# Two diagonals for the slots' maxima, POOL started by VectorE's first tile, and token maxima broadcast through DRAM in a soft-MoE dispatch

## What is computed

```
xn = rmsnorm(x, norm_gamma);  sn = rmsnorm(slot_embeds, slot_norm_gamma)
logits = einsum('bnd,esd->bnes', xn, sn)              # 2048 tokens x (8 experts x 128 slots)
dispatch = softmax(logits, axis=1)                    # over the tokens, one sum for each slot
combine = softmax(logits.reshape(b, n, e * s), -1)    # over the slots, one sum for each token
slots = einsum('bnd,bnes->besd', xn, dispatch)
h = gelu(einsum('besd,edh->besh', slots, w1) + b1)
eo = einsum('besh,ehd->besd', h, w2) + b2
out = einsum('bmd,bnm->bnd', eo, combine)
```

## Time and profile before

| what | value |
|---|---|
| time, median of 3 runs | 3299.77 us (3297.85 to 3300.67) |
| profiled execution | 3297.0 us |
| its span in the trace | 3295.2 us |
| mean granted clock of PE | 0.981 |
| busy: PE, PEld, DVE, ACT, POOL | 93%, 47%, 68%, 54%, 10% |
| instructions | 45435 |

### The profile page before, as it was taken

The page is one execution under the profiler, slowest core; times in us unless marked ns, Lnnn a source line. Parts: engine busy times, 40 slices in busy tenths (PEclk is TensorE's granted clock), DMA queues, the critical chain, the costliest instruction groups (busy, mean ns, idle before and its releaser), DMA issues.

```text
span 3295.2 us, 45435 instructions
## 1 busy us (share of the span) xinstructions
PE 3071.7 (93%) x17679; PEld 1544.8 (47%) x17679; DVE 2252.1 (68%) x4403; ACT 1763.6 (54%) x3199; POOL 329.8 (10%) x193
## 2 busy tenths in 40 slices
PE   5799999999889999998989999999997999999899
PEld 2433334447553333453854333344575433334468
DVE  4788887562678888756368888856546888885632
ACT  2366666564236666645514666654540566665560
POOL 3200000210400000111130000012122000002200
PEclk9799999999999999999999999999999999999999
DMA  4322201015502220002542202000443220100052
GB/s 129 99 40 40 40 2 39 14 52 197 149 20 40 40 40 27 20 7 95 190 119 46 39 9 40 27 20 7 151 163 103 40 41 11 31 27 27 9 179 81
DMA packets 123555, 201.89 MB, mean 61 GB/s; under 512 B 10094, under 2 KB 106996, under 8 KB 120232
## 3 DMA queue, kind: packets, MB, share of 16 engines
q1 hardware_dynamic: 110820, 148.58, 13.9%
q10 hardware_dynamic: 12520, 50.40, 8.2%
HBM read 156.01 MB, written 42.16 MB: 60 GB/s over the span
## 4 chain that ended last, share of the span: by engine, by line
PE 74%; DVE 17%; ACT 4%; issue 2%; POOL 1%; DMA 1%; ACTq 0%; SPq 0%; DVEq 0%; POOLq 0%
PE ps L694 14%; DVE pm L1269 12%; PE ps L674 10%; PE ps L614 9%; PE ps L795 7%; PE ps L850 7%; PE ps L627 6%; PE ps L881 3%; PE ps L870 3%; PE ps L574 2%; PE ps L738 2%; PE ps L659 2%; PE ps L678 1%; PE ps L808 1%; PE ps L603 1%
## 5 line engine op out<-in xcount | busy, mean ns | idle before, releaser
L1269 DVE TENSOR_REDUCE pm<-ps 128x1 f32<-128x512 f32 (+4 forms) x2560 | 1376.9, 602 | 273.6 <-PE ps L614 181.9
L983 ACT ACTIVATE R<-ps 128x512 f32<-128x512 f32 (+1 forms) x2240 | 1175.5, 593 | 603.0 <-PE ps L674 412.1
L674 PE MATMUL ps<-R 99*128 99x512 bf16 (+3 forms) x2560 | 827.9, 349 | 10.7 <-ACT R L983 6.0
L614 PE MATMUL ps<-R 96*128 96x512 bf16 x1536 | 578.6, 387 | 46.2 <-DVE pm L1269 40.7
L694 PE MATMUL ps<-R 128*17 128x512 f32 (+3 forms) x5120 | 528.9, 531 | 0.0
L614 PEld LDWEIGHTS ps<-R 96*128 96x128 bf16 x1536 | 147.3, 97 | 446.4 <-DVE pm L1269 372.0
L674 PEld LDWEIGHTS ps<-R 99*128 99x128 bf16 x2560 | 241.4, 97 | 146.0 <-ACT R L983 64.1
L694 PEld LDWEIGHTS ps<-R 128*17 128x17 f32 x5120 | 117.8, 96 | 280.1 <-issue 168.3
L850 PE MATMUL ps<-R 128*128 128x512 f32 x512 | 231.7, 610 | 14.0 <-ACT R L1050 13.9
L627 PE MATMUL ps<-R 128*128 128x257 f32 x1024 | 237.4, 388 | 4.1 <-ACT R L934 3.6
L795 PE MATMUL ps<-snT,R 128*128 128x512 f32 x512 | 230.1, 593 | 0.0
(11 more groups left out here) (151 smaller groups left out, 3321.7 us busy)
## 6 DMA issues: line engine op xcount, KB each, us to landing
R<-in_L_ffn_w_dram SPq DMA_DIRECT2D x64, 1024.0 KB, 5.8
R<-q_parts ACTq DMA_DIRECT2D x12, 768.0 KB
R<-k_parts ACTq DMA_DIRECT2D x12, 768.0 KB
R<-in_L_attn_x_dram SPq DMA_DIRECT2D x16, 512.0 KB, 8.4
q_parts<-R SPq DMA_DIRECT2D x16, 512.0 KB, 3.6
k_parts<-R SPq DMA_DIRECT2D x16, 512.0 KB, 3.4
R<-in_L_attn_x_dram SPq DMA_DIRECT2D x4, 2048.0 KB, 8.3
x_park<-R SPq DMA_DIRECT2D x16, 512.0 KB, 2.6
```

Of the source, the lines that this page charges most:

```text
L614: last = mm(ps[:, bank, :], qt(4 * c + r), kt(4 * kc, 4), start=True, stop=True)
L674: last = mm(bank[:, i * w:(i + 1) * w], kst[g % 2][0:BROWS, h0 + i, j * P:(j + 1) * P], qst[g % 2][0:BROWS, h0 + i, (c + 1) * CH - w:(c + ...
L983: A(Eb[s % ESLOTS][:, h0:h0 + n, 0:w], ps[:, u % NST, 0:n * w].rearrange("p (n w) -> p n w", n=n), ACT.Exp, scale=SCALE).then_inc(s_ex, 1)
L1269: mx = lambda o, i: V.tensor_reduce(o, i, AX.X, ALU.max)
```

## The change

Five things are changed, and the other lines only follow in their counts:

1. `build_diag` has a second buffer: diagonal 1 (and the second of the sums) goes into `wogT`, whose own use is over by then. Neither of a pair waits for PE.
2. The last three token maxima (tiles 13 to 15) are taken behind the two diagonals of the slots' maxima, ahead of DVE's first add.
3. POOL begins its adds once DVE has finished that of tile 0.
4. Broadcasts 2 to 5 and their diagonals are gone. In their place PE turns `negc` (128 x 16) behind tile 1, ACT copies the 16 x 128 values into `negcT` behind the exponential of tile 1, and SP stores them in DRAM (8 KB), waits, and loads them back as one row of 2048 values into all partitions. DVE waits for that load (`s_ncl`) ahead of its first shift of `EcT`.
5. The broadcasts of the sums are numbered 3 and 4.

```diff
+    negc_park = nc.dram_tensor("negated_token_maxima", (NT, P), f32, kind="Internal").ap()
+        negcT = sb("negcT", [NT, P])
+        diags = [diag[:, :, :], wogT[:, :, :].rearrange("p k (a t) -> p (k a) t", t=P)]
 SP
+                sp.wait_ge(s_be, b * 5 + 3)
+                sp.dma_start(negc_park, negcT[:, :]).then_inc(s_ncp, 16)
+                sp.wait_ge(s_ncp, b * 16 + 16)
+                sp.dma_start(negcb, negc_park.rearrange("(o t) p -> o (t p)", o=1).to_broadcast([P, T])).then_inc(s_ncl, 16)
 PE
                 def broadcast(i):
-                    pe.wait_ge(s_dg, b * 8 + i + 1)
+                    if i == 2:
+                        pe.wait_ge(s_Lm, b * NT + NT)
+                    else:
+                        pe.wait_ge(s_dg, b * 4 + (i + 1 if i < 2 else i))
                     if i >= 2:
-                        pe.wait_ge(s_be, b * 8 + i - 1)
-                    mm(ps[:, 4 + i % 2, :], ones[:, :], diag[:, :, :].rearrange("p r t -> p (r t)"),
-                       start=True, stop=True).then_inc(s_bc, 1)
+                        pe.wait_ge(s_be, b * 5 + i - 1)
+                    if i == 2:
+                        tr(ps[0:NT, 4, 0:P], negc[:, :], ident[:, :]).then_inc(s_bc, 1)
+                    else:
+                        mm(ps[:, 4 + i % 2, :], ones[:, :], diags[i in (1, 4)].rearrange("p r t -> p (r t)"),
+                           start=True, stop=True).then_inc(s_bc, 1)
...
-                    if 1 <= n <= 4:
-                        broadcast(n + 1)
-                broadcast(6)
-                broadcast(7)
+                    if n == 1:
+                        broadcast(2)
+                broadcast(3)
+                broadcast(4)
 ACT
+                    if i == 2:
+                        nc.scalar.copy(negcT[:, :], ps[0:NT, 4, 0:P]).then_inc(s_be, 1)
...
-                    if 2 <= n <= 5:
-                        broadcast(n)
-                broadcast(6)
-                broadcast(7)
+                    if n == 1:
+                        broadcast(2)
+                broadcast(3)
+                broadcast(4)
 POOL
-                pool.wait_ge(s_be, b * 8 + 2)
+                pool.wait_ge(s_eds, b * 11 + 1)
+                pool.wait_ge(s_be, b * 5 + 2)
                 for n in range(2, NT, 3):
+                    pool.wait_ge(s_Lm, b * NT + n + 1)
 DVE
-                for n in range(NT):
+                def token_max(n):
                     dve.wait_ge(s_Lc, b * 16 + n + 1)
                     V.tensor_reduce(negc[:, n:n + 1], L[:, n, :], AX.X, ALU.max, negate=True).then_inc(s_Lm, 1)
+                late = 3
+                for n in range(NT):
+                    if n < NT - late:
+                        token_max(n)
...
-                    if i:
-                        dve.wait_ge(s_bc, b * 8 + i)
-                    V.tensor_tensor(out=diag[:, :, :], in0=ident[:, :].unsqueeze(1).to_broadcast([P, 4, P]),
+                    if i > 2:
+                        dve.wait_ge(s_bc, b * 5 + i - 2)
+                    V.tensor_tensor(out=diags[i in (1, 4)], in0=ident[:, :].unsqueeze(1).to_broadcast([P, 4, P]),
...
                 build_diag(negM[:, 0:4], 0)
                 build_diag(negM[:, 4:8], 1)
+                for n in range(NT - late, NT):
+                    token_max(n)
...
-                    if 1 <= n <= 4:
-                        build_diag(negc[:, 4 * n - 4:4 * n], n + 1)
...
-                            dve.wait_ge(s_be, b * 8 + 6)
+                            dve.wait_ge(s_ncl, b * 16 + 16)
```

More of the change, by code:

```diff
@@ L378, in adaln_block @@
         s_be = sem("broadcast_evacuated")
+        s_ncp = sem("token_maxima_parked")
+        s_ncl = sem("token_maxima_broadcast")
         s_ltc = sem("logitsT_copied")
@@ L883, in expert_out @@
                     last.then_inc(s_y, 1)
-                pe.wait_ge(s_be, b * 8 + 8)
+                pe.wait_ge(s_be, b * 5 + 5)
                 hidden(0)
@@ L1033, in broadcast @@
                 def broadcast(i):
[L1034 to L1038, removed]
-                    else:
-                        dst = rdb[:, (i - 6) * 512:(i - 5) * 512]
-                    nc.scalar.copy(dst, ps[:, 4 + i % 2, :]).then_inc(s_be, 1)
+                    act.wait_ge(s_bc, b * 5 + i + 1)
+                    if i == 2:
+                        nc.scalar.copy(negcT[:, :], ps[0:NT, 4, 0:P]).then_inc(s_be, 1)
+                    else:
+                        dst = negMb[:, i * 512:(i + 1) * 512] if i < 2 else rdb[:, (i - 3) * 512:(i - 2) * 512]
+                        nc.scalar.copy(dst, ps[:, 4 + i % 2, :]).then_inc(s_be, 1)
                 act.wait_ge(s_L, b * 16 + 16)
@@ L1467, in _ @@
                 build_diag(negM[:, 4:8], 1)
-                dve.wait_ge(s_be, b * 8 + 2)
+                for n in range(NT - late, NT):
+                    token_max(n)
+                dve.wait_ge(s_be, b * 5 + 2)
                 for n in range(NT):
@@ L1482, in _ @@
                 link(V.reciprocal(dsum[:, :], dsum[:, :]))
-                build_diag(dsum[:, 0:4], 6)
-                build_diag(dsum[:, 4:8], 7)
-                dve.wait_ge(s_be, b * 8 + 8)
+                build_diag(dsum[:, 0:4], 3)
+                build_diag(dsum[:, 4:8], 4)
+                dve.wait_ge(s_be, b * 5 + 5)
                 dve.wait_ge(s_slh, b + 1)
```

## The result

The changed kernel takes 3286.81 us (median of 6 runs, 3281.32 to 3294.64), the kernel before beside it 3298.81 us. The forecast was 17.3 us and 3282.5 us. The direction is right and the time lies in the range, but a third of the gain is missing. The profiled execution took 3285.36 us, with a span of 3283.5 us, against 3295.2.

The account below looks back on a forecast made before the run. TensorE, with 74% of the chain of waits, was taken as the bound. Gains of 4.3 + 6.8 + 2.0 + 4.2 = 17.3 us, against a median of 3299.77, gave 3282.5 us, range 3276 to 3292.

Parts of the forecast that it names:

- Start: Before the first add: moved token maxima and two diagonals gain 0.83 us in batch 0, 1.15 in each other, 4.3 together.
- Broadcasts gone: Dispatch: four broadcasts go, a transpose and stall of 1.75 us a batch come, gaining 6.8 us; waits for tile 3 go, 2.0.
- End: Sums' two broadcasts ahead of the experts: both diagonals ready, 1.05 us less a batch, 4.2 in all, passed on whole.
- DRAM: Maxima's trip through DRAM: the row lands at 710, at worst 720, before VectorE must have it at 723.6; cost 0.
- Rival (c): At VectorE's first shift of turned logits: a DRAM trip over 20.4 us costs time, at 30 giving 3321; chance 0.04.
- POOL: Early adds: VectorE's first add precedes POOL's anyway, then the two alternate; POOL starting behind VectorE's first tile costs 0.
- Clock at the start: First two tiles: half clock from 688.7 to 698.3 loses 8.4 us over four batches; left as it is, ± 4.
- (a): Behind tile 1: the new 1.4 us gap drops TensorE's clock, costing 1.6 to 3.0 us a batch, 3290.9; chance 0.13.

Follow-up runs that it names:

- e7: The change with all token maxima back in their old places (late = 0): 3283.05 us, ratio 0.9955 to the kernel before.
- e4: The change with the transpose of the token maxima and its copy moved ahead of tile 0: 3277.86 us, ratio 0.9937 to the kernel before.
- e2: The kernel before with only the second buffer for diagonals added: 3289.12 us, ratio 0.9974 to the kernel before.
- e9: e6 without POOL's wait for VectorE's first tile: 3265.96 us, ratio 0.9912 to the kernel before.
- e6: e4 plus 26 matmuls of ones by ones in TensorE's idle time at the dispatch's start: 3271.77 us, ratio 0.9929 to the kernel before.
- e3: The change's DRAM path alone, with one diagonal buffer, token maxima and POOL's start as before: 3294.77 us, ratio 0.9988 to the kernel before.
- e11: The kernel before, unedited, one execution for a second trace: 3301.08 us.
- e10: The change with 14 matmuls of ones by ones in TensorE's two gaps ahead of the experts: 3274.98 us, ratio 0.9934 to the kernel before.
- e12: e6 plus the edits of e10, with VectorE and POOL adding in fixed turns: 3261.15 us, ratio 0.9896 to the kernel before.
- e1: The change again, unedited, timed and traced a second time: 3286.29 us, ratio 0.9963 to the kernel before.
- e5: The change with five matmuls of ones by ones filling TensorE's gap behind tile 1: 3281.94 us, ratio 0.9950 to the kernel before.

## Why the prediction was right and where it was wrong

By its own steps, from the profiled execution of the change against that of before:

- **Start, 4.3 us.** The first adds start 5.25, 4.59, 5.02 and 4.85 us behind diagonal 0; before it was 5.44, 6.29, 6.01 and 5.99. That is 4.0. I had batch 0 wrong (0.83 forecast, 0.19 measured), since its first broadcast ran at half clock this time (2.05 us, not 1.10), and batch 1 the other way round (1.15 forecast, 1.70 measured). The three moved maxima cost the first add up to 0.63 us where the clock is full (e7), as the step had them.
- **Broadcasts gone, 6.8 and 2.0 us.** Transpose to tile 2 takes 1.57 us in all four batches (forecast 1.75; the copy is 0.25, the transpose 0.27). Tile 3 no longer waits. e4 shows the cause of the stall: moved into a gap, it goes.
- **End, 4.2 us.** From the first of the last two broadcasts to the scaled slots it is 1.05 us less in each batch. e2 has start and end together at 8.6, forecast 8.5.
- **DRAM, 0.** 5.6 to 6.3 us for the trip in the change's three traces, and TensorE never waits for it. Rival (c) did not come.
- **POOL, 0.** Right for the change as a whole, but not for the reason given. I argued that VectorE's first add goes ahead of POOL anyway; with three token maxima ahead of that add it doesn't, and without its wait POOL takes 1.1 us a batch from tile 0 (e9). And the adds don't reliably alternate, which I took from one pair: VectorE ran six in one piece in three of the change's twelve batches and in all four of e6.
- **Clock at the start.** The prediction let it stand, within 4 us either way. The first two tiles took 37.2 us over the four batches, 36.5 before. Its times of the fall were misread: a granted clock of 0.69 in the window from 688 to 689 puts the fall at 688.4, not 688.7, and the return at 698.6, not 698.3. Its 8.4 us lost is 8.5. Neither bears on the sum.

The dispatches are 292.1 - 275.2 = 16.9 us shorter, 18.7 and 17.6 in the other two traces, against 17.3. **The step that failed is the last half sentence of the end term**: "the first expert output starts 10.85 us after that copy ..., whatever the clock of the hidden matmuls, so this gain passes on whole". In the change it does start there (10.80 to 10.82 us behind the start of the scaling in all twelve batches), but the clock of what comes behind it was not counted. Nor does it hold whatever the clock: with hidden matmuls of over 10 us the output came 0.9 us late in two batches of e3 and 1.1 in one of the kernel before itself (e11). TensorE has two gaps there, 2.12 us ahead of the hidden matmuls and 1.93 ahead of the first output if those ran at full clock. In two traces of before the clock was down during the hidden matmuls, which ScalarE covers up to some 9.3 us, in five of eight batches, and never in the first output. In three traces of the change it was down in the first output in seven of twelve, at 1.69 us each and, in the third trace, another 1.2 before the next attention. Filling both gaps (e10) takes 11.5 us from the change. In all traces without this filling the clock fell in one or the other of the two stages in 35 of 48 batches; with it (e10, e12) in none of eight.

How far this explains what is missing (5 to 7 us: 17.3 forecast, 10 and 12 measured by the two ratios): from the first output to the next attention it takes 190.1 us on average in the change's three traces (nine batches, 188.4 to 191.4) and 189.4 in the two of before (six, 188.8 to 189.8), and from the last scaled slots to the end 122.9 and 121.9. That makes 3 us a run, the size of the 2.5 us by which the rest of the span is longer. The other half is not in the traces: they average 3284.0 us, 2.5 below the change's median, and the longest executions (3291 to 3295) were not traced. They have the lower clock, though: 0.983 on average in the two fastest of e1, 0.980 in the slowest of all (3294.64), and 0.003 of the span is 10 us, an estimate of what that can cost at most.

Of the rivals, (a) had the right kind of cause, a gap that brings the clock down, and looked in the wrong place. By the Trainium skill (TensorE: Matmul & The Clock Gate, section "Part 1: The HAM clock gate"), throttled is the default and activity releases it. The traces agree: e6 only adds activity to e4, and the first two tiles take 7.1 us for 8.8 to 9.5 (8.7 to 10.1 in the change). In the prediction I used the rule for the gap that the change adds, and not for those that were there already and whose distance from the last fall it moves.

What stays open: why the half clock falls on the hidden matmuls in the one kernel and on the output in the other. The traces show that it does, and e10 that the gaps are needed for it. The length of the dispatch may decide it: at 70.7 to 71.0 us (e2) and at 66.6 to 67.0 (e4) it fell on the hidden matmuls in all eight batches; in the change, at 68.1 to 70.0, on the output in seven, on the hidden matmuls in one and on neither in four. But in the change the output was hit at 68.26 us and spared at 68.38 and 68.41, and no run moved the length by itself. Open too is what e5 and e7 gain, and a part of e10's gain: the first outputs account for 6.8 of its 11.5 us (half clock in 7 of 12 batches, so 2.33 a run, at 2.9 each), and the change's traced executions were 2.5 us faster than its median.

## What to carry to other kernels

Where an engine's clock depends on what it did before, an idle gap is not free even if another engine sets its end: ask what runs right behind it, and whether that is covered. Before a chain is shortened, look at the stages behind it for gaps of that engine, and try to fill them with work that costs nothing. Two engines that hold each other up, as VectorE and POOL do here, can be given a fixed turn (e12); an alternation that is seen in one trace may be an accident. And a trace is one execution: set its time beside the median of its kernel before a difference of a few us is read from it.

## What was not expected of the hardware

- A gap of 1.93 us on TensorE, 7.4 us of matmuls behind another of 2.12, was followed by half clock in 7 of 11 batches in the change's three traces, while the new one of 1.30 us was not in any of twelve.
- Back to back adds of VectorE kept POOL from its own for 7 us and more: 1.15 us for each of VectorE's, and POOL's add, 2.3 us alone, ended 11 us after its start (e6, ScalarE's wait of 6.8 us). With VectorE's wait behind its second add, as in e12, it took 3.3.
- A kernel's own spread follows the clock: of the change's twelve runs the three fastest (3279.5 to 3281.3 us) had a mean granted clock of 0.982 to 0.983, the four slowest (3290.9 to 3294.6) 0.980 to 0.981.
